# A cross-attention block over two contexts: its weights levelled ahead, its biases as products, its tiles and values inside the first pass

## What is computed

```python
def _ln(t, w, b):
    m = jnp.mean(t, axis=-1, keepdims=True)
    v = jnp.var(t, axis=-1, keepdims=True)
    return (t - m) * jax.lax.rsqrt(v + EPS) * w + b

kv_dca = (y_dca @ Wkv_dca + bkv_dca).reshape(b, DCA, 2, H, HD)
k_dca = _ln(kv_dca[:, :, 0], kn_dca_w, kn_dca_b)
v_dca = kv_dca[:, :, 1]
q = _ln((x @ Wq + bq).reshape(b, s1, H, HD), qn_w, qn_b)
kv = jnp.concatenate([y_main @ Wk + bk, y_main @ Wv + bv], axis=-1)
kv = kv.reshape(b, s2, H, 2 * HD)
k = _ln(kv[..., :HD], kn_w, kn_b)
v = kv[..., HD:]
ctx = _attn(q, k, v) + _attn(q, k_dca, v_dca)
x = x + (ctx @ Wo + bo)
```

## Time and profile before

| what | us |
|---|---|
| median of 3 runs | 2254.58 (2253.4 to 2258.34) |
| the profiled execution, its own time | 2261.51 |
| its span | 2258.4 |
| TensorE busy (share of the span) | 1882.2 (83%) |
| VectorE busy | 1258.1 (56%) |
| ScalarE busy | 781.3 (35%) |
| GpSimd busy | 262.9 (12%) |
| mean granted TensorE clock | 0.909 |
| the changed block in the trace | 1107.47 to 1302.8 |

### The profile page before, as it was taken

One profiled execution on the slowest core, in us unless ns is written; L12 is line 12 of the kernel. 1 busy time (PEld: TensorE's weight loads), 2 busy tenths in 40 slices (PEclk: granted clock), 3 DMA queues, 4 the chain that ended last, 5 costly groups with the idle time before them and its releaser, 6 DMA issues.

```text
span 2258.4 us, 25459 instructions
## 1 busy us (share of the span) xinstructions
PE 1882.2 (83%) x9051; PEld 1205.4 (53%) x9056; DVE 1258.1 (56%) x2847; ACT 781.3 (35%) x1837; POOL 262.9 (12%) x250
## 2 busy tenths in 40 slices
PE   6684766978579699999757858999999899998698
PEld 3451223645455366666544536555555477777455
DVE  5738998654763444444586586333334666665222
ACT  4215454204432233333421512333333455554111
POOL 2711000000104100000110110000000222220111
PEclk9896788999869799999866979999999999999799
DMA  3000000000451200000100031100000200001310
GB/s 146 1 28 29 0 0 20 1 28 2 191 210 61 90 1 1 1 1 1 38 0 1 2 150 61 70 1 1 1 0 16 99 1 1 1 1 66 111 31 15
DMA packets 17371, 83.38 MB, mean 37 GB/s; under 512 B 3136, under 2 KB 9924, under 8 KB 13152
## 3 DMA queue, kind: packets, MB, share of 16 engines
q1 hardware_dynamic: 11168, 71.61, 8.0%
q0 software_dynamic: 2944, 8.03, 1.2%
q10 hardware_dynamic: 3136, 2.13, 0.3%
HBM read 73.49 MB, written 8.81 MB: 36 GB/s over the span
## 4 chain that ended last, share of the span: by engine, by line
PE 69%; DVE 17%; issue 6%; ACT 3%; POOL 3%; DMA 1%; another core or an unknown queue 0%; POOLq 0%; DVEq 0%; SPq 0%; ACTq 0%
PE bank L136 56%; PE bank L141 8%; PE bank L3379 3%; DVE space L795 2%; PE bank L3401 2%; DVE space L784 1%; DVE space L2930 1%; DVE space L1359 1%; DVE space L178 1%; DMA space<-in_L_attn 1%; POOL space L625 1%; POOL space L639 1%; ACT space L2985 0%; DVE space L189 0%; DVE space L272 0%
## 5 line engine op out<-in xcount | busy, mean ns | idle before, releaser
L136 PE MATMUL bank<-space 128*128 128x256 f32 (+15 forms) x6725 | 1456.1, 426 | 103.3 <-DVE space L2930 19.1
L136 PEld LDWEIGHTS bank<-space 128*128 128x128 f32 (+7 forms) x6730 | 892.0, 183 | 617.3 <-issue 389.8
L141 PE MATMUL bank<-consts,space 128*128 128x128 f32 (+2 forms) x1602 | 257.8, 304 | 189.6 <-DVE space L189 58.9
L141 PEld LDWEIGHTS bank<-consts,space 128*128 128x128 f32 (+2 forms) x1602 | 206.3, 155 | 255.9 <-issue 132.1
L136 PE MATMUL bank<-space,consts 128*128 128x512 f32 (+1 forms) x132 | 82.7, 757 | 57.3 <-DVE space L790 50.2
L197 POOL TENSOR_TENSOR space<-space,consts 128x4 f32<-128x4 f32 x22 | 24.9, 1131 | 684.2 <-DVE space L184 684.2
L2620 POOL TENSOR_TENSOR space<-space,consts 128x4 f32<-128x4 f32 x64 | 68.6, 1071 | 218.1 <-DVE space L2551 218.1
L2415 ACT ACTIVATE space<-bank,space 128x256 f32<-128x256 f32 x128 | 59.4, 469 | 95.7 <-DVE space L2369 95.7
L2369 DVE TENSOR_REDUCE space<-bank 128x2 f32<-128x512 f32 x64 | 44.0, 688 | 86.8 <-PE bank L136 86.6
L3379 PE MATMUL bank<-space 128*128 x176 | 80.7, 603 | 3.1 <-DVE space L3529 1.6
L2543 DVE TENSOR_REDUCE space<-bank 128x2 f32<-128x512 f32 x64 | 44.2, 691 | 69.2 <-PE bank L136 69.1
(11 more groups left out here) (349 smaller groups left out, 1975.5 us busy)
## 6 DMA issues: line engine op xcount, KB each, us to landing
space<-in_L_ffn SPq DMA_DIRECT2D x13, 2048.0 KB, 12.3
space<-in_L_attn SPq DMA_DIRECT2D x10, 2048.0 KB, 13.0
space<-in_L_xattn SPq DMA_DIRECT2D x4, 2048.0 KB, 10.1
expert_results<-space SPq DMA_DIRECT2D x16, 128.0 KB, 2.9
space<-expert_results SPq DMA_DIRECT2D x8, 256.0 KB, 4.4
space<-in_L_xattn SPq DMA_DIRECT2D x1, 1919.0 KB, 19.5
space<-in_L_xattn SPq DMA_DIRECT2D x1, 1536.0 KB, 6.1
space<-in_L_attn SPq DMA_DIRECT2D x1, 1074.5 KB, 5.0
```

Of the source, the lines that this page charges most:

```text
L136: return self.nc.tensor.matmul(out, lhsT, rhs, start=first, stop=last, skip_group_check=True)
L141: return self.nc.tensor.transpose(out, src, eye)
```

## The change

In words:

- The weights and biases of queries, keys and second keys are packed together as `level`, seven groups of 256 columns. GpSimd subtracts from each head's 16 columns their mean, in the weights themselves. It does so in the block before (`Causal`), from the moment that they are loaded. A product with them is already centred, so the sums, the means and GpSimd's subtraction go.
- The bias enters as a product of a row of ones with the bias row, the first in each unit's accumulation.
- The keys' units come first, two of them before x is transposed; the queries' come last. ScalarE squares straight from the bank, and copies keys to `raw` so that their banks are free; the query banks are read by the spread product itself.
- ScalarE blanks only the pad columns. GpSimd's clearing of `kd` and `rows_` is put behind the norm.
- Only the first half of the keys' and queries' tiles (batches 0 and 1) is transposed ahead of the scores. The other half, the values, the second keys, the second values and the output bias are made inside the pass over the maxima, in the order `FIRST`: scores 0, scores 1, keys, scores 2, queries, scores 3, values, scores 4, second keys, scores 5, turn 0, scores 6, second values, scores 7, bias, scores 8, scores 9, turn 1, and from there scores and turns as before. There are 26 positions; even ones use banks 0 to 3, odd ones banks 4 to 7. A position waits, bank by bank, for whoever reads the banks of two positions before.
- ScalarE takes the late tiles, the values and the second keys (in 4 pieces). The values' biases leave `v` and `vd`; their sum goes through `Wo` into the output bias `bo`.

The diff, cut to its core:

```diff
@@ Causal
+        self.following, self.scratch = None, c.sb(7 * D)
     def gpsimd(self, e):
         self.normed.gpsimd(e)
+        if self.following is not None:
+            self.following.level(e, self.scratch)
         e.wait_ge(*self.ld.all)
@@ TwoContexts
-    TILES = [(g, f) for g in range(0, 2 * NT, 4) for f in range(XH * XD_PAD // P)]
+    BESIDE = {1: ("keys", 1), 2: ("queries", 1), 3: ("values", 0), 4: ("second_keys", 0), 6: ("second_values", 0), 7: ("bias", 0)}
+    for u_ in range(19):
+        if u_ >= 6 and u_ % 4 == 2:
+            FIRST.append(("turn", u_ // 4 - 1))
+        if u_ < 16:
+            FIRST.append(("scores", u_))
+        if u_ in BESIDE:
+            FIRST.append(BESIDE[u_])
-        self.units = [u for i in range(0, NT, 2) for u in ((i, 2, P), (NT + i, 2, P))] + [(2 * NT, 1, self.ROWS)]
+        self.units = [(NT + i, 2, P, 4 + i // 2) for i in range(0, NT, 2)] + [(2 * NT, 1, self.ROWS, 4)]
+        self.units += [(i, 2, P, 4 + (i // 2 + 1) % 4) for i in range(0, NT, 2)]
+    def level(self, e, scratch):
+        heads = self.w["level"].rearrange("p a (h e) -> p (a h) e", e=XD)
+        e.wait_ge(*self.ld.all)
+        src, at, n = heads, 0, XD
+        while n > 1:
+            n //= 2
+            dst = scratch[:, at:at + heads.shape[1] * n].rearrange("p (h e) -> p h e", e=n)
+            nc.gpsimd.tensor_tensor(dst, src[:, :, 0:n], src[:, :, n:2 * n], ALU.add).then_inc(*c.g.next())
+            e.wait_ge(*c.g.so_far)
+            src, at = dst, at + heads.shape[1] * n
+        mean = src[:, :, 0]
+        nc.gpsimd.tensor_scalar(mean, mean, 1.0 / XD, None, ALU.mult).then_inc(*c.g.next())
+        e.wait_ge(*c.g.so_far)
+        nc.gpsimd.tensor_tensor(heads, heads, spread(mean, XD), ALU.subtract).then_inc(*self.s.levelled.one)
+    def unit(self, e, n):
+        if n >= 4:
+            e.wait_ge(*s.kept(n - 3))
+        c.mm(out[0:r, 0:k * D].rearrange("p (a b) -> p a b", b=D), c.ones[0:1, 0:r], repeat(w["level"][0:1, bias, :], k), True, False)
...
     def tensor(self, e):
+        e.wait_ge(*s.levelled.all)
+        for n in range(2):
+            self.unit(e, n)
+        self.x_turned.tensor(e, self.norm.s.normed)
+        for n in range(2, 5):
+            self.unit(e, n)
+        self.x_turned.wait(e, 0)
+        self.x_turned.wait(e, 1)
+        for n in range(5, 9):
+            self.unit(e, n)
+        e.wait_ge(*s.blank.all)
+        e.wait_ge(*s.centred(2))
+        for f in range(4):
+            self.turn_tile(bk[f], NT, f).then_inc(*s.tile.one)
+        e.wait_ge(*s.centred(7))
+        for f in range(4):
+            e.wait_ge(*s.tile_by_scalar(f + 1))
+            self.turn_tile(bk[f], 0, f).then_inc(*s.tile.one)
...
     def scores(self, e, p, u):
+        mine = self.half_of_banks(p)
+        if p == 1:
+            e.wait_ge(*self.s.centred.all)
+        if u == 8:
+            e.wait_ge(*t.late_tile.all)
         for i in range(TPB):
             for j in range(4):
+                if i == 0:
+                    self.wait_half(e, p, j)
...
     def vector(self, e):
+        for n in range(5):
+            self.add_squares(e, n)
+        for m in range(2):
+            self.mean_squares(e, m, 4 + m)
+        for m in range(2):
+            self.invert(e, m)
+        for n in range(5):
+            self.scale_unit(n)
+        for n in (5, 6):
+            self.add_squares(e, n)
+        self.mean_squares(e, 2, 7)
+        self.invert(e, 2)
+        for n in (5, 6):
+            self.scale_unit(n)
+        for n in (7, 8):
+            self.add_squares(e, n)
+        self.mean_squares(e, 3, 9)
+        for f in (1, 3):
+            e.wait_ge(*s.tile(5 + f))
+            nc.vector.tensor_scalar(dst[:, f, 0:HALF], bk[f], wb[:, 0:1], wb[:, 1:2], ALU.mult, ALU.add).then_inc(
+        self.invert(e, 3)
+        for n in (7, 8):
+            self.scale_unit(n)
         self.maxima(e)
...
     def scalar(self, e):
+        blanks = [padded[:, n:min(n + P, padded.shape[1]), XD:] for n in range(0, padded.shape[1], P)] + [v[:, :, XD + 1:]]
+        for n in range(2):
+            self.square(e, n)
         self.x_turned.scalar(e)
+        for n in range(2, 5):
+            self.square(e, n)
+        for m in range(2):
+            self.take_root(e, m)
+        for n in range(5, 8):
+            self.square(e, n)
+        self.take_root(e, 2)
+        self.square(e, 8)
...
     def gpsimd(self, e):
+        if not self.levelled_ahead:
+            self.level(e, flat(self.q))
         self.norm.gpsimd(e)
+        e.wait_ge(*self.norm.s.normed.all)
         nc.gpsimd.memset(self.kd.rearrange("p a b c -> p (a b c)"), 0.0).then_inc(*s.kd_clear.one)
```

More of the change, by code:

```diff
@@ L2678, in __init__ @@
-            dca_turned=1, dca_ready=1, v_mm=4, v_ready=4, many_ready=4, vd_mm=4, vd_ready=4)
+            levelled=1, scaled=2, blank=4, many_ready=B, ones_ready=1, rows_clear=1, kd_clear=1, product=n, kept=5, squared=n, summed=n, var=4,
+            root=4, inverted=4, centred=n, tile=8, tile_by_vector=2, tile_by_scalar=6)
         self.t = c.signals(
-            scores=16, maxed=64, rows_turned=B, q_done=B, st_mm=16, exped=64, mixed=16, raw_ready=16, use=uses, taken=uses,
-            second_exp=B, second_ready=B, o_ready=NT)
@@ new lines, in unit @@
+    def unit(self, e, n):
+        c, w, s = self.c, self.w, self.s
+        i, k, r, bank = self.units[n]
+        out = c.banks[bank]
+        bias = 4 if i < NT else 5 if i < 2 * NT else 6
+        if n >= 4:
+            e.wait_ge(*s.kept(n - 3))
+        c.mm(out[0:r, 0:k * D].rearrange("p (a b) -> p a b", b=D), c.ones[0:1, 0:r], repeat(w["level"][0:1, bias, :], k), True, False)
+        for j in range(k):
+            half = out[0:r, j * D:(j + 1) * D]
+            if i < NT:
+                for m in range(DC):
+                    done = c.mm(half, self.xT[:, m, (i + j) * P:(i + j + 1) * P], w["level"][:, m, :], False, m == DC - 1)
+            elif i < 2 * NT:
+                at = (i - NT + j) * P
+                done = c.mm(half, w["ctxT"][:, 0, at:at + P], w["level"][:, 2, :], False, True)
+            else:
+                done = c.mm(half, w["dcaT"], w["level"][:, 3, :], False, True)
+        done.then_inc(*s.product.one)
@@ new lines, in turn_tile @@
+    def turn_tile(self, bank, g, f):
+        for i in range(4):
+            done = self.c.turn(bank[:, i * P:(i + 1) * P], self.padded[:, g + i, f * P:(f + 1) * P])
+        return done
+    def tensor(self, e):
+        c, w, s, t, bk = self.c, self.w, self.s, self.t, self.c.banks
+        e.wait_ge(*self.ld.all)
+        e.wait_ge(*s.levelled.all)
+        for n in range(2):
+            self.unit(e, n)
+        self.x_turned.tensor(e, self.norm.s.normed)
+        for n in range(2, 5):
[12 more added lines that the diff above has]
+            self.turn_tile(bk[f], 0, f).then_inc(*s.tile.one)
+        e.wait_ge(*s.tile_by_scalar.all)
@@ L2735, in attention @@
         N = len(self.UNITS)
[L2736 to L2740, removed]
+        for p, (kind, at) in enumerate(self.FIRST):
+            if kind == "scores":
+                self.scores(e, p, at)
+            elif kind == "turn":
+                self.turn_rows(e, p, at)
+            else:
+                self.beside(e, p, kind)
         n = 0
@@ new lines, in take_tile, with square @@
+    def take_tile(self, g, f, bank):
+        dst, wb = self.tile(g)
+        at = g % NT * P
+        return self.c.nc.scalar.activation(dst[:, f, at:at + HALF], bank, ACT.Identity, scale=wb[:, 0:1], bias=wb[:, 1:2])
+    def square(self, e, n):
+        c, s, nc = self.c, self.s, self.c.nc
+        i, k, r, bank = self.units[n]
+        e.wait_ge(*s.product(n + 1))
+        src = c.banks[bank][0:r, 0:k * D]
+        if n >= 4:
+            e.wait_ge(*s.summed(n - 3))
+        nc.scalar.activation(self.tmp[n % 4][0:r, 0:k * D], src, ACT.Square).then_inc(*s.squared.one)
+        if i >= NT:
+            nc.scalar.activation(flat(self.raw[0:r, i:i + k, :]), src, ACT.Copy).then_inc(*s.kept.one)
```

363 lines of the change are left out of this document (183 added, 180 removed).

## The result

The changed kernel takes 2225.95 us (median of 4 runs, 2215.88 to 2233.82) against 2253.99 for the kernel before (4 runs, 2250.82 to 2258.34): a ratio of 0.986, 95% interval 0.984 to 0.988. Its own runs spread over 18 us, more than twice the spread of the kernel before. The experiments found two sources, of 3 to 5 us each; they don't account for all of it.

The account below looks back on a forecast made before the run. Relays between engines, none full, bound the first phase and the maxima. Gains of 33.9 and 2.8 us, less 2.5 for handovers, gave 34.2: from a median of 2254.58 to 2220.4 us, range 2212 to 2234.

Parts of the forecast that it names:

- rival with the dear bias products: One-row bias products before the first maximum each take 0.89 us longer, 4.8 us in all; time 2225; chance 8%.
- Ahead of the block: GpSimd levels weights and biases in the block before: about 7.4 us of work, cost taken as 0.
- GpSimd slows the block before: Levelling stretches VectorE's work in the preceding block by 2.3 us at most; time 2222.7; chance 3%.
- Blanking and norm: At the block's start: blanking only pad columns takes about 5.8 us; clearing put behind the norm gains 2.0 us.
- Products: Query and key units: 0.89 us per one-row bias product; key units 1.8, query units 2.7, ending at 24.4 us.
- Clock: TensorE's run from 9.3 to 24.4 us has no hole, so it was priced at full clock.
- the bias products cost the double: Between 9.3 and 24.4 us, each bias product takes 0.89 us longer, 4.8 us counted; time 2225; chance 8%.
- First tiles: Only eight key and query tiles stand ahead of the scores; first maximum at 31.5 us instead of 65.4, gain 33.9.
- Maxima: From the first maximum to the second pass: 52.8 us instead of 55.6, gain 2.8.
- the pass over the maxima grows: TensorE at half clock from unit 1 to 8 makes the pass 64 us, not 52.8; time 2231.5; chance 12%.
- Tables: ScalarE's squares between roots might need three more table loads of 1.283 us, about 1 us on the path.
- The signs named ahead: Profile checks: block 159 us, first maximum at 31.5, second pass at 84, normalising 2.8, surrounding blocks within 1 us.

Follow-up runs that it names:

- again: The changed kernel run once more, unaltered, with a second profile: median 2226.22 us, ratio 0.9862 to the kernel before.
- late_first: The changed kernel with all late work (tiles, values, second keys, second values, bias) moved from the pass over the maxima to ahead of the first scores: median 2225.99 us.

## Why the prediction was right, point by point

The direction, the phase and the rough size were right: of the forecast 33.9 us before the first maximum, 27.4 came in the profiled execution and 31.1 in "again"; of the 2.8 in the pass, 3.1 (52.4 against 55.5). The measured median, 2225.95, lies in the range, though nearer to the time of the rival with the dear bias products (2225) than to the forecast (2220.4).

- *Ahead of the block.* Levelling costs the block before nothing (354.29 us with it, 354.52 without). Its price was 8.1 instead of 7.4, and putting it inside costs 10.5. So the rival *GpSimd slows the block before*, which the forecast calls sure by the rule alone, cost nothing here.
- *Blanking and norm.* The norm took 2.83 as forecast. But the 2.0 us of gain was no gain: TensorE's first two units, the second of them at half clock, last until 6.0 us behind the start (I had 3.5), and the transposes come behind them. The step that began unit 2 at 9.3 was right to a tenth in the profiled execution (1117.78 is 9.3) by luck: a start 0.7 later and transposes 0.7 shorter than I took. In "again" that unit starts at 10.4.
- *Products.* This is the term that was mis-sized. I took 0.89 for a one-row product and 1.76 for a query unit's four; that is what full-row products cost (0.86 and 1.72). Measured with one row: 1.05 and 1.93. From 9.3 us to the end of the query units "again" takes 18.3 us instead of 15.1. Of these 3.2 us, 1.1 are the later start of unit 2 and 2.1 the units themselves (17.2 us): the changes of row count add some 2.7 (0.4 in six units, 0.3 in the second keys'), and full-row prices would have been 0.6 below my sum.
- *Clock.* "No hole, so full clock" failed in the profiled execution, and so did "the clock rises in every dense stretch": 10 us at half clock came between 12.4 and 22.7. From unit 2 to the first maximum it takes 28.7 us and "again" 23.9, so they cost 4.8, of which 3.7 are left at the first maximum because unit 2 starts 1.1 earlier. The rival *the bias products cost the double* had the place and the size (4.8), but as a price per product (1.05 at full clock, not 1.9); it was the clock. The Trainium skill (TensorE: Matmul & The Clock Gate, "Part 1: The HAM clock gate (the "warmup" mystery)") says the gate follows how busy TensorE has been; by busy time alone, as the profile shows it, the stretch at 9.80 of 9.80 would be at full clock, and the measurement differs.
- *First tiles.* From the end of the query units to the first maximum: forecast 7.1 us, measured 6.7 in "again".
- *Maxima.* Forecast 52.8, measured 52.4, with two errors that offset: VectorE's work was about 42 us instead of 43.7 (a unit behind another takes 2.30, not 2.38), and its waits 8.4 instead of 7.0, with 2.35 before unit 4 where I had 1.7. The rival *the pass over the maxima grows* didn't come; TensorE was busy 16.99 of 17.50 us at clock 1.00 there.
- *Tables.* Two loads. The three more, about 1 us of them on the path, didn't come.
- *The signs named ahead.* Right: the normalising instructions (2.8 us), the second pass (90.5, in 80 to 95), TensorE without a hole from 9 to 24 us, VectorE's waits before units 2 to 5, two table loads. Missed: the first maximum at 38.0 (29 to 35), the clock from 9 to 24 us (0.66 in the profiled execution, 0.99 in "again", where I had 0.9 or more), the block (164.9 for 159), and the blocks around, which moved by up to 2.8 us where I had 1.

The share of single parts, which the forecast didn't give, can be read in part by comparing the kernel before with late_first. In both, all tiles and values stand ahead of the scores. Before the first maximum late_first is 21.3 us shorter (44.1 against 65.4) and in the pass 11.9 (43.7 against 55.5). The 21.3 hold the two early key units (4.2), blanking and clearing (at most 0.5), and what VectorE and GpSimd no longer do per unit (bias adds, means, centring) together with the new order; that this last share is the largest is what is left over, not tested by itself. The 11.9 go with the two halves of the banks. Moving the late work inside gives only 1 to 2 us more, which is why the changed kernel's pass, at 52.4, looks nearly unchanged.

## What to carry to other kernels

When a relay is removed, look at which engine is busy without a hole afterwards and price everything on it, small operands too: here the bias products are some 9 of the 27.6 us up to the end of the query units in "again" (8.5 times 1.05, an estimate). A product with one row cost what one with 128 rows cost (0.86 us), plus 0.2 for the change on either side; use all rows. And filling waits with work that needs the same banks hides little: the pass gave back in bank waits nearly all that it hid. Compare a changed stretch with one of the same content: only the run with the late work outside showed that the pass itself had become 11.9 us shorter.

## What the runs showed that was not expected

TensorE's granted clock fell from 1.00 to 0.50 in a stretch without holes (9.80 busy of 9.80 us) where one-row products alternated with full ones. Such a stretch came in four of eight executions, and the clock stayed low for most of 59 us (mean 0.63) where the one-row products were tripled. With the tripled products streamed over 128 rows, of which 127 carry zero weights, it was 1.00 up to the first maximum, in the one execution profiled. A change between one-row and 128-row products cost about 0.2 us at full clock. And the unchanged second pass has two lengths, 71.2 to 72.0 us at a mean clock of 0.98 to 0.99 or 74.1 to 74.5 at 0.93, whatever was edited ahead of it. The long one runs at half clock for its first 10 to 11 us, again without a hole (10.7 of 10.7 us busy in the changed kernel's first profile); what picks one of them stays open.
